# A two-layer transformer kernel: the second attention's out-projection, the last norm and the expert routing are laid into the attention, and the dispatch scatters wait after every eighth

## The chip, the cores and the metric

The kernel is one program on one core of a Trainium2 chip. Its engines are TensorE (PE, with its weight loads as PEld), VectorE (DVE), ScalarE (ACT), GpSimd (POOL) and SyncE (SP), which here issues most DMAs. The metric is the device time of one execution in microseconds (us), lower is better. The kernel before took 1064.49 us, the median of three runs (1061.39 to 1065.01).

## The reference, cut to what matters

Input x has 16 sequences of 256 tokens, 128 features: 4096 tokens. Two layers; each is an attention-like part and an expert part, both behind a layer norm with a scale and a shift per sequence, and both added back through a gate per sequence.

```python
h = _layernorm(x) * (1 + ca) + sa
x = x + ga * _L1_attn_ref(h, ...)     # 16 heads of 8, causal, relative positions, out = ctx @ w_o.T
h = _layernorm(x) * (1 + cb) + sb
x = x + gb * _L1_ffn_ref(h, ...)
# _L1_ffn_ref
gates = softmax(relu(xf @ Wr1 + br1) @ Wr2 + br2);  tg, ti = top_k(gates, 2)
out = silu(xf @ Ws1 + bs1) @ Ws2 + bs2              # shared expert, hidden 512
for e in range(8):
    out += w_e[:, None] * (silu(xf @ We1[e] + be1[e]) @ We2[e] + be2[e])
```

The first layer (a scan and eight small experts) is not touched by the change.

## The kernel before, in words

The work is cut in eight *chunks* of 512 tokens, two sequences each; for the attention of layer 1 a chunk is called a *pair*. The order of each engine's instructions is written out by hand, and semaphores join the engines.

**Attention.** `pair(i, k)` on PE runs 24 score banks twice: a first round whose row maxima DVE takes (`maxima`, L1188), a second whose exponentials ACT takes (`exponentials`, L799). Between the banks of the first round PE weights the values of pair i-1 (`weighted_values`, `weighted_relative`), and in the second it computes the relative scores of pair i+1, which DVE turns into bias tables (`bias_out`, L1178 and L1180). SP moves maxima (`move_maxima`), stores the contexts to DRAM (`store_values`, `store_relative`; the sums of the exponentials are one of nine rows of a head) and loads the next pair.

**Out-projection.** After all pairs SP loads sums, contexts and relative contexts back into SBUF (L540 to L554). DVE takes the reciprocal of the sums, PE spreads it over the features with a selecting matmul (`selp`, L1659), GpSimd adds the two contexts (`join`, L666), DVE multiplies (L1232), PE projects (L1671), DVE gates (`gated`, L948), GpSimd adds to x (`residual`, L618), and DVE takes mean and variance of a token (`statistics`, L888 and L891).

**Last norm and routing.** `layer_norm(3, ...)`: one square root for all tokens (ACT), normalised chunks (DVE, L936), transposes (PE, L1400), scale and shift (ACT, L728); with it the router: hidden layer (PE, L1699), transposed rows back (PE, L1681), logits (PE, L1711). Per group of two chunks DVE picks the two experts (`choose(g)`, L1013 to L1259), PE sums ranks over tokens (`ranks(g)`, L1688 and L1689), and DVE makes row numbers (`destinations(g)`, L1265 to L1271).

**Dispatch.** For each group g and each of the two picks k GpSimd issues eight indirect DMAs (scatters, L689) that write rows of x to their experts' places in DRAM: 64 scatters of 128 rows.

**Shared expert** (PE L1731 up, L1742 down; ACT L844 the silu; DVE L1318, L956, L959), then **experts**: 39 tiles of 256 rows, loaded by SP (L570, L573) once all scatters have landed, the shared expert is done and the tile table is there; GpSimd scatters the results (L697). Then a last stage weights and adds the two results of a token and stores the output.

Of the kernel before, what the change touches and what calls it, by code (L numbers as in the profile page):

```python
# [18 lines left out]
U32 = mybir.dt.uint32  # L19
ALU = mybir.AluOpType  # L20
# [3 lines left out]
P = 128  # L24
# [3 lines left out]
CH = 512  # L28
# [12 lines left out]
RANK_AT = 2  # L41
# [33 lines left out]
def build(nc, A, out):  # L75
    ctx = ExitStack()
    with ctx:
# [94 lines left out]
        R = Region(moe_base)  # L172
        Wr1 = R.take(32)
        Wr2 = R.take(E)
        br1 = R.take(1)
        RT1 = R.take(2 * CH).rearrange("p (s n) -> p s n", s=2)
        rowid = R.take(2 * NT).rearrange("p (k t) -> p k t", k=2)
        steps = R.take(2 * 64).rearrange("p (k n) -> p k n", k=2)
        below = R.take(P)
        restart = R.take(GE)  # L180
        reach = R.take(E * KT).rearrange("p (e k) -> p e k", e=E)
        ME, IN, EX = [R.take(NE).rearrange("p (g e t) -> p g e t", g=GROUPS, e=E) for _ in range(3)]
        tot = R.take(GROUPS * E).rearrange("p (g e) -> p g e", g=GROUPS)
        cum = R.take((GROUPS + 1) * E).rearrange("p (g e) -> p g e", g=GROUPS + 1)
        tiles, upto, spare = [R.take(E) for _ in range(3)]
        cmp, cmpd = [R.take(64 * E) for _ in range(2)]
        dest = [R.take(NT).bitcast(U32) for _ in range(2)]
        texp, tbase = [R.take(NG) for _ in range(2)]
        texpu, tbaseu = [R.take(NG).bitcast(U32) for _ in range(2)]
        ROWS = [R.take(NT * RW).rearrange("p (t n) -> p t n", t=NT) for _ in range(2)]  # L190
        W1S = R.take(W1W)
        W1 = R.take(UT * W1W).rearrange("p (s n) -> p s n", s=UT)
        moe_units = R.at
        HM1 = R.take(2 * KB1 * CH).rearrange("p (s k n) -> p s k n", s=2, k=KB1)
        R = Region(moe_units)
        HMT = R.take(2 * KB1 * GT).rearrange("p (s k n) -> p s k n", s=2, k=KB1)
        XR = R.take(UT * 2 * RW).rearrange("p (s r n) -> p s r n", s=UT, r=2)
        rid = R.take(UT * 2).rearrange("p (s r) -> p s r", s=UT).bitcast(U32)
        XT = R.take(2 * GT).rearrange("p (s n) -> p s n", s=2)
        YS = R.take(UT * GT).rearrange("p (s r n) -> p s r n", s=UT, r=2)  # L200
        YG = [r.rearrange("p t n -> p (t n)")[:, 0:NT * D].rearrange("p (t n) -> p t n", t=NT) for r in ROWS]


# [17 lines left out]
        BH, BL = [[R.take(P // 2 * BQ, BF16).rearrange("p (m q) -> p m q", q=BQ) for _ in range(2)] for _ in range(2)]  # L221
        PT = R.take(HS * PX).rearrange("p (h q) -> p h q", h=HS)
# [20 lines left out]
        R = Region(0)  # L243
        C1 = R.take(TOK)
        R1 = R.take(TOK)
        R = Region(early)
        DN = R.take(CH)
        DR = R.take(CH)
        DN7, DR7 = R.take(CH), R.take(CH)
        CX = R.take(2 * CH).rearrange("p (s n) -> p s n", s=2)  # L250
        selp = R.take(NP * P).rearrange("p (c n) -> p c n", c=NP)
        woT1 = R.take(D)
# [7 lines left out]
        rD = scratch("context_rel", [P, TOK])  # L260
        xsD = scratch("dispatched_rows", [AREA + SPARE * GT, RW])
# [54 lines left out]
        s_din7 = sem("s_din7")  # L316
# [23 lines left out]
        s_cin = [sem(f"s_cin{k}") for k in range(3)]  # L340
# [35 lines left out]

        def rank_bank(g):
            return bank[2 if g < 2 else 7]
# [12 lines left out]
        def _(sp):  # L391
# [136 lines left out]
            load_pair(1, 1)  # L528
            move_maxima(0, 0, 0)
# [5 lines left out]
            sp.wait_ge(s_r2, 24 * NP)  # L535
            for s, k in ((s_cst[0], 16 * 8), (s_cst[1], 16 * 8), (s_rst, 16 * 32)):
                sp.wait_ge(s, k * (NP - 1))
            part = (NP - 1) * CH
            values = cD.rearrange("(h v) t -> h v t", v=VW)
            sp.dma_start(DN[0:H * (NP - 1), :], values[:, HD, 0:part].rearrange("h (c t) -> c h t", c=NP - 1)  # L540
                         ).then_inc(s_din, 16)
            sp.dma_start(selp[:, :, :], A["selp"]).then_inc(s_wo, 16)
            sp.dma_start(woT1[:, :], A["woT1"]).then_inc(s_wo, 16)
            for k, (lo, hi) in enumerate(((0, 2 * CH), (2 * CH, part))):
                sp.dma_start(C1[:, lo:hi], values[:, 0:HD, lo:hi]).then_inc(s_cin[k], 16)
                sp.dma_start(R1[:, lo:hi], rD[:, lo:hi]).then_inc(s_cin[k], 16)
            store_values(NP - 1)
            for k in range(2):
                sp.wait_ge(s_cst[k], 16 * 8 * NP)
# [55 lines left out]
        def _(pool):  # L605
# [53 lines left out]
            for i in range(NP):  # L659
                neighbours(i)  # L660
                pool.wait_ge(s_nb, 2 * i + 2)
# [1250 lines left out]
```

## Time and profile before

| | us |
|---|---|
| median of three runs | 1064.49 |
| profiled execution, its own time | 1063.62 |
| its span, first to last instruction | 1061.6 |
| first layer, and the second's projections | 0 to 392 |
| attention, eight pairs | 392 to 655.2 |
| contexts back, out-projection, statistics | 655.2 to 708 |
| norm, routing, shared expert (and scatters, 737.8 to 829.9) | 708 to 858.6 |
| 39 expert tiles | 858.6 to 1029.7 |
| weighting, output | 1029.7 to 1061.6 |

PE is busy for 82% of the span, DVE for 57%, ACT for 33%, GpSimd for 23%. An average over the span hides the stages: PE has almost no idle time in the attention and with the expert tiles, and a good deal between the two. Times of the rows below are counted from the span's start.

### The profile page before, as it was taken

The numbers are of one execution on the slowest core, as the hardware profiler recorded it, in microseconds if no ns is written. First come the engines' busy times: TensorE is split into PE (matmuls) and PEld (weight loads), VectorE is DVE, ScalarE is ACT, GpSimd is POOL, SyncE is SP. The second block draws the span as 40 slices with busy tenths as digits, with TensorE's granted clock in tenths as the row PEclk, the third lists the DMA queues.
The fourth block names the chain that finished last, engine by engine and source line by source line (L and its number), as shares of the span: only waits on it lengthen the run. The fifth ranks groups of instructions, "written<-read, shape, count | busy, mean of one in ns | idle before, by whom it ended". The sixth has DMA issues, their size and how long they took to land.

```text
span 1061.6 us, 22575 instructions
## 1 busy us (share of the span) xinstructions
PE 870.2 (82%) x8768; PEld 601.6 (57%) x8768; DVE 608.5 (57%) x1613; ACT 352.2 (33%) x672; POOL 249.1 (23%) x251
## 2 busy tenths in 40 slices
PE   4875598999959699999999999855558879999960
PEld 3665265666635455665666565533336568888850
DVE  8781767666777887767776771474323222222217
ACT  1422021222241214553455345124121334344323
POOL 1030000000345400000000000521756204454443
PEclk9985699999979759999999996968578889999995
DMA  7993000000025712312231213610111036777747
GB/s 220 345 319 105 0 8 8 8 15 7 0 112 157 210 53 54 69 29 67 63 69 27 68 25 70 153 47 8 53 40 43 18 110 195 206 220 218 215 122 210
DMA packets 110363, 105.34 MB, mean 99 GB/s; under 512 B 47476, under 2 KB 100661, under 8 KB 109333
## 3 DMA queue, kind: packets, MB, share of 16 engines
q1 hardware_dynamic: 105733, 94.79, 32.2%
q0 software_dynamic: 4544, 9.35, 2.5%
q8 instruction: 60, 0.98, 0.4%
q14 instruction: 26, 0.21, 0.1%
HBM read 79.39 MB, written 44.51 MB: 117 GB/s over the span
## 4 chain that ended last, share of the span: by engine, by line
PE 60%; DVE 17%; issue 6%; DMA 6%; SPq 4%; ACT 3%; POOL 2%; another core or an unknown queue 1%; DVEq 0%; POOLq 0%
PE bank L1760 7%; PE bank L1770 6%; PE bank L1609 5%; PE bank L1447 5%; PE bank L1458 4%; PE bank L1459 4%; PE bank L1551 4%; PE bank L1503 4%; DVE sb_arena L1188 4%; PE bank L1742 3%; PE bank L1731 3%; PE bank L1529 3%; PE bank L1534 2%; DMA sb_arena<-in_iota 2%; SPq L470 1%
## 5 line engine op out<-in xcount | busy, mean ns | idle before, releaser
L1188 DVE TRANSPOSE_TENSOR_REDUCE sb_arena<-bank 128x16 f32<-128x512 f32 x192 | 120.4, 686 | 22.9 <-PE bank L1551 21.5
L799 ACT ACTIVATE sb_arena<-bank 128x512 f32<-128x512 f32 x192 | 99.1, 603 | 48.3 <-PE bank L1551 48.3
L697 POOL DMA_INDIRECT expert_results<-sb_arena x78 | 74.6, 957 | 125.1 <-DVE sb_arena L1340 109.6
L854 ACT ACTIVATE sb_arena<-bank,sb_arena 128x256 f32<-128x256 f32 x156 | 65.3, 472 | 102.4 <-PE bank L1760 101.7
L1447 PEld LDWEIGHTS bank<-sb_arena 128*128 128x128 f32 x512 | 67.3, 194 | 47.4 <-issue 25.4
L756 ACT ACTIVATE sb_arena<-bank 128x512 f32<-128x512 f32 x64 | 38.2, 597 | 151.2 <-PE bank L1459 151.2
L1760 PE MATMUL bank<-sb_arena 128*128 128x256 f32 x312 | 80.5, 402 | 6.7 <-DMA sb_arena<-in_w 2.7
L1447 PE MATMUL bank<-sb_arena 128*128 128x128 f32 x512 | 69.4, 279 | 16.1 <-DVE sb_arena L1099 16.1
L689 POOL DMA_INDIRECT dispatched_rows<-sb_arena x64 | 62.3, 973 | 62.6 <-DVE sb_arena L1271 44.0
L1770 PE MATMUL bank<-sb_arena 128*128 128x128 f32 x624 | 75.9, 274 | 0.0
L1081 DVE SCALAR_TENSOR_TENSOR sb_arena<-bank,sb_arena 128x128 f32<-128x128 f32 x256 | 71.7, 342 | 3.0 <-PE bank L1447 3.0
L1099 DVE TENSOR_TENSOR sb_arena<-sb_arena,bank 128x512 f32<-128x512 f32 x64 | 43.7, 685 | 51.4 <-ACT sb_arena L756 51.2
L1770 PEld LDWEIGHTS bank<-sb_arena 128*128 128x128 f32 x624 | 72.8, 191 | 0.1
L1609 PE MATMUL bank<-sb_arena 128*16 128x128 f32 x1024 | 68.0, 421 | 0.9 <-issue 0.9
L1760 PEld LDWEIGHTS bank<-sb_arena 128*128 128x128 f32 x312 | 58.1, 196 | 18.6 <-issue 9.1
L1458 PE MATMUL bank<-sb_arena 128*128 128x512 f32 x128 | 67.4, 609 | 0.0
L1503 PE MATMUL bank<-sb_arena 128*128 128x56 bf16 (+1 forms) x512 | 62.2, 281 | 5.5 <-DVE sb_arena L1168 3.2
L1459 PE MATMUL bank<-sb_arena 128*128 128x512 f32 x128 | 66.6, 602 | 0.0
L1178 DVE CAST sb_arena<-bank 128x512 bf16<-128x512 f32 x64 | 44.1, 689 | 38.5 <-PE bank L1503 38.5
L1551 PE MATMUL bank<-sb_arena,sb_identb 128*32 128x128 bf16 (+1 forms) x2304 | 64.9, 247 | 0.4 <-DVE sb_arena L1178 0.4
L1334 DVE CAST sb_arena<-sb_arena 128x2 uint32<-128x2 f32 x39 | 6.9, 178 | 98.6 <-DMA expert_results<-sb_arena 82.3
L652 POOL COPY sb_arena<-sb_arena 32x1024 f32<-32x1024 f32 x8 | 8.3, 1038 | 232.8 <-ACT sb_arena L799 232.8
(231 smaller groups left out, 1452.0 us busy)
## 6 DMA issues: line engine op xcount, KB each, us to landing
sb_arena<-in_w SPq DMA_DIRECT2D x39, 578.0 KB
dispatched_rows<-in_padding SPq DMA_DIRECT2D x8, 2064.0 KB, 34.9
sb_arena<-dispatched_rows SPq DMA_DIRECT2D x39, 129.0 KB
sb_GATE<-gates SPq DMA_DIRECT2D x2, 2048.0 KB, 7.1
sb_arena<-q_parts SPq DMA_DIRECT2D x8, 512.0 KB, 3.7
sb_arena<-k_parts SPq DMA_DIRECT2D x8, 512.0 KB, 5.1
context_rel<-sb_arena SPq DMA_DIRECT2D x256, 8.0 KB
sb_arena<-expert_results SPq DMA_DIRECT2D x16, 256.0 KB, 5.3
```

The source lines that it names most:

```text
L697: nc.gpsimd.indirect_dma_start(yD[:, :], bass.IndirectOffsetOnAxis(ap=rid[:, k, r:r + 1], axis=0), YS[:, k, r, :], None).then_inc(s_yo[k], 16)
L799: nc.scalar.activation(dst, src, ACT.Exp).then_inc(s_ex, 1)
L1081: ins = v.scalar_tensor_tensor(out=ACC[:, T, :], in0=src[:, t * D:(t + 1) * D], scalar=wstep[:, (j // NC) % 2, T:T + 1], in1=ACC[:, T, :], ...
L1188: v.tensor_reduce(dst.rearrange("p h b -> p (h b)"), bank[r % RING][:, :].rearrange("p (b c) -> p b c", c=32), AX, ALU.max, apply_transpos ...
L1447: ins = mm(bank[4 + j % 2][:, t * D:(t + 1) * D], HM0[:, j % 2, t * P:(t + 1) * P], W0[:, k, 2 * F0:3 * F0], start=True, stop=True)
L1458: mm(bank[j % 2][:, :], W0[:, k, 0:F0], chunk(hT, c), start=True, stop=True)
L1459: mm(bank[2 + j % 2][:, :], W0[:, k, F0:2 * F0], chunk(hT, c), start=True, stop=True).then_inc(s_up[0], 1)
L1503: ins = mm(out[:, :, :, x], GT4[:, first:first + 32, :].rearrange("p x a -> p (x a)"), queries[:, :, :, q], start=True, stop=True, skip_gr ...
L1551: ins = mm(dst[32 * b:32 * b + 32, :, 32 * b:32 * b + w], identb[:, 32 * a:32 * a + 32], src[:, :, :].rearrange("p (g b) q -> p g b q", g= ...
L1609: ins = mm(out[32 * j:32 * j + 2 * HD, :, x], relk[:, 32 * j + 8 * w + 2 * x:32 * j + 8 * w + 2 * x + 2, :], four, start=True, stop=True, ...
L1760: ins = mm(bank[2 * (k % 2) + b // 2][:, b % 2 * GT:(b % 2 + 1) * GT], W1[:, k, b * P:(b + 1) * P], XT[:, k % 2, :], start=True, stop=True ...
L1770: ins = mm(bank[6 + k % 2][:, r * D:(r + 1) * D], HMT[:, k % 2, b, r * P:(r + 1) * P], W1[:, k, I1 + b * D:I1 + (b + 1) * D], start=(b == ...
```

## The change

Nothing of the computation is changed but where the reciprocals of the sums are taken and how they are spread. What moves:

1. **Out-projection inside the attention.** `context_in(j)` on SP, right behind the stores of pair j, loads that pair's sums (as 128 x 64), its contexts and relative contexts, writes the reciprocals to DRAM and reads them back spread over the features, so the selecting matmul is gone. `context(j)` on GpSimd adds and multiplies, `project(j)` on PE stands in the second round of pair j+2, `gate_out(j)`, `sums(j+1)` and `statistics1(j)` stand in DVE's stream of pair j+2, `residual1(j)` in GpSimd's. So chunks 0 to 5 are done when the last pair's scores are.
2. **Norm and routing of chunks 0 to 5 beside the weighting of the last pair**, then the shared expert of the first chunks before chunks 6 and 7 have been normalised. The order is written out call by call on PE, ACT and DVE. The scatters start after `destinations(0)`, as before, and run beside the shared expert.
3. **GpSimd waits** before each group of eight scatters until all scatters so far have landed.

```diff
+            def context_in(j):
+                for k in range(2):
+                    sp.wait_ge(s_cst[k], 16 * 8 * (j + 1))
+                at = j * CH
+                values = cD.rearrange("(h v) t -> h v t", v=VW)[:, :, at:at + CH]
+                wait(sp, s_dr, j)
+                sp.dma_start(DN[:, :], values[:, HD, :].rearrange("h (s q) -> h s q", s=8)).then_inc(s_din, 16)
+                store_relative(j)
+                sp.wait_ge(s_dr, j + 1)
+                sp.dma_start(sD[j].rearrange("h (s q) -> (h s) q", s=8), DR[:, :]).then_inc(s_dst, 16)
+                if j >= 2:
+                    sp.wait_ge(s_y, NC + j - 1)
+                sp.dma_start(C1[:, j % 2, :], values[:, 0:HD, :]).then_inc(s_cin, 16)
+                sp.wait_ge(s_rst, 16 * 32 * (j + 1))
+                wait(sp, s_cr, j)
+                sp.dma_start(R1[:, :], rD[:, at:at + CH]).then_inc(s_cin, 16)
+                sp.wait_ge(s_dst, 16 * (j + 1))
+                wait(sp, s_cx, j)
+                sp.dma_start(DB[:, :], sD[j].unsqueeze(1).to_broadcast([H, HD, CH])).then_inc(s_db, 16)
...
                 load_values(i)
-                store_relative(i - 1)
+                context_in(i - 1)
...
             store_values(NP - 1)
...
+            context_in(NP - 1)
+            sp.wait_ge(s_rl, 4 * NP)
+            sp.wait_ge(s_nb, 2 * NP)
             sp.dma_start(W1S[:, :], A["w1s"]).then_inc(s_sw, 16)
...
             for i in range(NP):
+                if i >= 2:
+                    context(i - 2)
+                    residual1(i - 2)
                 neighbours(i)
...
                 for k in range(2):
+                    if g or k:
+                        pool.wait_ge(s_disp, 16 * GN * (2 * g + k))
                     pool.wait_ge(s_dest, 2 * g + k + 1)
                     for t in range(g * GN, (g + 1) * GN):
                         nc.gpsimd.indirect_dma_start(
...
                 if not last:
-                    bias_out(i + 1, 1 - k, range(1, BG))
+                    bias_out(i + 1, 1 - k, range(1, 4))
+                if i >= 2:
+                    gate_out(i - 2)
+                if not last:
+                    bias_out(i + 1, 1 - k, range(4, 6))
+                if i >= 1:
+                    sums(i - 1)
+                if not last:
+                    bias_out(i + 1, 1 - k, range(6, BG))
+                if i >= 2:
+                    statistics1(i - 2)
...
+            for c in range(5):
+                normalise1(c)
+            gate_out(6)
+            choose(0)
+            statistics1(6)
+            normalise1(5)
+            destinations(0)
+            choose(1)
+            sums(7)
+            last_context(7)
             destinations(1)
-            for g in range(2, GROUPS):
-                choose(g)
-                destinations(g)
+            choose(2)
+            gate_out(7)
+            last_residual(7)
+            statistics1(7)
+            destinations(2)
...
+            choose(3)
+            shared_out(4)
+            destinations(3)
...
+                    if part == 1 and i >= 2:
+                        pe.wait_ge(s_nm, 2 * i + 2)
+                        project(i - 2)
```

On DVE at the end of a pair in the middle of the attention, before (names: L1178 and L1180 are the bias tables, L1188 the first maxima of the next pair):

```order
L1178 CAST sb_arena<-bank5 128x64x8 [waits s_gen]
L1180 TENSOR_TENSOR sb_arena<-bank5,sb_arena 128x64x8 [waits s_bh]
L1178 CAST sb_arena<-bank6 128x64x8 [waits s_gen]
L1180 TENSOR_TENSOR sb_arena<-bank6,sb_arena 128x64x8 [waits s_bh]
L1188 TENSOR_REDUCE sb_arena<-bank0 128x16 [waits s_r1]
```

and now (L1261 and L1263 are the bias tables, L1312 the sums' reciprocal, L964 and L967 the statistics, L1271 the maxima):

```order
L1312 RECIPROCAL sb_arena<-sb_arena 128x64 [waits s_dst,s_din]
L1261 CAST sb_arena<-bank5 128x64x8 [waits s_gen]
L1263 TENSOR_TENSOR sb_arena<-bank5,sb_arena 128x64x8 [waits s_bh]
L1261 CAST sb_arena<-bank6 128x64x8 [waits s_gen]
L1263 TENSOR_TENSOR sb_arena<-bank6,sb_arena 128x64x8 [waits s_bh]
L964 BN_STATS sb_ST<-sb_X 128x6 [waits s_yr]
L964 BN_STATS sb_ST<-sb_X 128x6 x3
L967 BN_AGGR sb_MV<-sb_ST 128x2 [waits s_dv]
L967 BN_AGGR sb_MV<-sb_ST 128x2 x3
L1271 TENSOR_REDUCE sb_arena<-bank0 128x16 [waits s_r1]
```

The statistics of pair i-2 stand between the last bias table and the next pair's first maxima, and wait for GpSimd's residual.

On PE after the last pair's scores, before (L1581 and L1585 weight the values, L1609 the relative part, L1659 and L1671 the out-projection, L1400 the norm's transposes):

```order
L1585 MATMUL bank<-sb_arena 9x128 x4
L1609 MATMUL bank<-sb_arena 16x128 x64
L1659 MATMUL bank<-sb_arena 128x512 x2
L1671 MATMUL bank<-sb_arena 128x128 x4
L1659 MATMUL bank<-sb_arena 128x512
```

and now (L1744 relative part, L1803 transposes of the norm, L1809 router's hidden layer, L1816 rows back, L1829 logits, L1840 ranks, L1858 and L1868 shared expert up and down, L1755 projection), from the end of the last pair's weighting on:

```order
L1744 MATMUL bank<-sb_arena 16x128 x16
L1803 MATMUL bank<-sb_ident,sb_arena 128x128 x4
L1809 MATMUL bank<-sb_arena 32x512
L1816 MATMUL bank<-sb_ident,sb_arena 128x128 x4
L1829 MATMUL bank<-sb_arena 128x8 x4
L1840 MATMUL bank<-sb_arena 128x8
...
L1858 MATMUL bank<-sb_arena 128x512 x8
L1755 MATMUL bank<-sb_arena 128x128 x4
L1868 MATMUL bank<-sb_arena 128x128 x16
```

The norm's transposes of chunk 5 now follow the last relative part, and the last projection stands behind the shared expert's first two chunks.

On GpSimd, a scatter group before, and now:

```order
L689 DMA dispatched_rows<-sb_arena 34560x129 [waits s_dest]
L689 DMA dispatched_rows<-sb_arena 34560x129 x7
L689 DMA dispatched_rows<-sb_arena 34560x129 [waits s_dest,s_rows]
L689 DMA dispatched_rows<-sb_arena 34560x129 x7
L689 DMA dispatched_rows<-sb_arena 34560x129 [waits s_dest]
```

```order
L725 DMA dispatched_rows<-sb_arena 34560x129 [waits s_dest,s_disp]
L725 DMA dispatched_rows<-sb_arena 34560x129 x7
L725 DMA dispatched_rows<-sb_arena 34560x129 [waits s_dest,s_disp,s_rows]
L725 DMA dispatched_rows<-sb_arena 34560x129 x7
L725 DMA dispatched_rows<-sb_arena 34560x129 [waits s_dest,s_disp]
```

Only the wait for `s_disp`, which counts landed scatters, is new.

## Rows read from the trace of the kernel before

**Rows 1.** Stages: length, busy us of PE, PEld, DVE, ACT, POOL, clock, DMA share, GB/s

```profile
392.00:655.20 263.20, 256.85 (x5407) 161.02 (x5399) 186.60 (x309) 134.74 (x247) 17.42 (x17) 0.97 0.24 50
655.20:708.00 52.80, 37.62 (x336) 23.15 (x336) 27.49 (x96) 7.64 (x12) 21.97 (x18) 0.76 0.52 124
708.00:858.60 150.60, 104.29 (x482) 69.31 (x482) 51.93 (x191) 48.88 (x81) 62.26 (x64) 0.77 0.09 29
858.60:1029.70 171.10, 156.79 (x1014) 140.37 (x1014) 40.22 (x124) 65.33 (x156) 74.64 (x78) 0.97 0.67 195
```

**Rows 2.** The chain that ended last, 655 to 860: start, us, what

```profile
667.86 12.82 DMA context<-sb_XN
...
769.35 13.61 another core or an unknown queue
```

**Rows 3.** Timeline of DVE: start, us, engine line op, idle before and releaser

```profile
585.54 7.72 DVE L1188 TRANSPOSE_TENSOR_REDUCE sb_arena<-bank 128x16 f32<-128x512 f32 x12
...
684.68 0.75 DVE L948 TENSOR_TENSOR sb_TMP<-bank,sb_GATE 128x256 f32<-128x256 f32 x2
...
687.81 0.87 DVE L888 BATCH_NORM_STATS2 sb_ST<-sb_X 128x6 f32<-128x128 f32 x4
688.72 0.38 DVE L891 BATCH_NORM_AGGREGATE sb_MV<-sb_ST 128x2 f32<-128x6 f32 x4
...
724.64 0.22 DVE L1017 TENSOR_REDUCE sb_arena<-sb_arena 128x8 f32<-128x64 f32 x1 [4.34 <-ACT sb_arena L827]
...
729.53 2.14 DVE L936 TENSOR_SCALAR sb_XN<-sb_X,sb_MV,sb_RSTD 128x128 f32<-128x128 f32 x8
...
783.06 0.22 DVE L1265 TENSOR_TENSOR sb_arena<-sb_arena,bank 128x64 f32<-128x64 f32 x1 [13.71 <-remote]
```

**Rows 4.** Timeline of PE

```profile
587.50 0.39 PE L1529 MATMUL bank<-sb_arena 32*128 32x256 bf16 x2 [0.21 <-DVE sb_arena L1188]
...
664.22 7.90 PE L1609 MATMUL bank<-sb_arena 128*16 128x128 f32 x125
...
687.44 1.05 PE L1671 MATMUL bank<-sb_arena 128*128 128x128 f32 x8
...
745.40 1.11 PE L1400 MATMUL bank<-sb_ident,sb_XN 128*128 128x128 f32 x4 [6.55 <-issue]
...
751.60 0.58 PE L1689 MATMUL bank<-sb_arena,sb_ones 128*128 128x8 f32 x2
...
770.72 0.58 PE L1689 MATMUL bank<-sb_arena,sb_ones 128*128 128x8 f32 x2
...
787.55 5.77 PE L1731 MATMUL bank<-sb_arena 128*128 128x512 f32 x8 [10.98 <-ACT sb_arena L844]
...
837.22 3.73 PE L1742 MATMUL bank<-sb_arena 128*128 128x128 f32 x32
840.79 3.60 PE L1731 MATMUL bank<-sb_arena 128*128 128x512 f32 x8
```

**Rows 5.** Timeline of ACT

```profile
705.47 1.28 ACT L723 ACT_TABLE_LOAD   x1 [31.14 <-DVE sb_MV L891]
```

**Rows 6.** The scatters as one group: busy us, mean ns of one, idle before

```profile
L689 POOL DMA_INDIRECT dispatched_rows<-sb_arena x64 | 62.3, 973 | 62.6 <-DVE sb_arena L1271 44.0 <-issue 18.6
```

**Rows 7.** Timeline of GpSimd

```profile
784.83 0.96 POOL L689 DMA_INDIRECT dispatched_rows<-sb_arena  x1 [6.62 <-DVE sb_arena L1271]
...
817.30 1.27 POOL L689 DMA_INDIRECT dispatched_rows<-sb_arena  x1 [0.30 <-issue]
...
1028.67 0.96 POOL L697 DMA_INDIRECT expert_results<-sb_arena  x1 [0.30 <-issue]
```

**Rows 8.** Timeline of SP's queue

```profile
859.61 0.40 SPq L570 DMA_DIRECT2D sb_arena<-dispatched_rows  x1
...
1031.04 9.54 SPq L595 DMA_DIRECT2D sb_arena<-expert_results  x12
```

**Rows 9.** DMA issues, 656 to 708: KB each, median us to landing

```profile
sb_arena<-in_w1s SPq DMA_DIRECT2D x1, 578.0 KB, 3.7
```

More of the change, by code:

```diff
@@ L171, in build @@
         moe0_end = R.at
[L172 to L201, printed above, removed]
         R = Region(dense_base)
@@ new lines, in build @@
+        EX = R.take(NE).rearrange("p (g e t) -> p g e t", g=GROUPS, e=E)
+        tot = R.take(GROUPS * E).rearrange("p (g e) -> p g e", g=GROUPS)
+        cum = R.take((GROUPS + 1) * E).rearrange("p (g e) -> p g e", g=GROUPS + 1)
+        tiles, upto, spare = [R.take(E) for _ in range(3)]
+        cmp, cmpd = [R.take(NG * E) for _ in range(2)]
+        dest = [R.take(NT).bitcast(U32) for _ in range(2)]
+        texp, tbase = [R.take(NG) for _ in range(2)]
+        texpu, tbaseu = [R.take(NG).bitcast(U32) for _ in range(2)]
@@ L339, in build @@
         s_rst = sem("s_rst")
-        s_cin = [sem(f"s_cin{k}") for k in range(3)]
+        s_cin = sem("s_cin")
+        s_dst = sem("s_dst")
         s_wo = sem("s_wo")
@@ L1281, in _ @@
+            dve.wait_ge(s_wm[1], 16 * 10)
+            inverse_deviations(3, 0, 6)
             for k in range(2):
@@ new lines, in shared_down @@
+            def shared_down(c):
+                pe.wait_ge(s_sact, (c + 1) * KB1)
+                if c == 0:
+                    pe.wait_ge(s_dest, 3)
+                wait(pe, s_sout, c - 1)
+                for t in range(TPC):
+                    for b in range(KB1):
+                        ins = mm(bank[4 + c % 2][:, t * D:(t + 1) * D], HM1[:, c % 2, b, t * P:(t + 1) * P],
+                                 W1S[:, I1 + b * D:I1 + (b + 1) * D], start=(b == 0), stop=(b == KB1 - 1))
+                ins.then_inc(s_sdn, 1)
@@ new lines, in _ @@
+            last = NP - 1
+            norm_transposes(0)
+            weighted_values(last, range(0, 4))
+            norm_transposes(1)
+            route_hidden(0)
+            back(0)
+            weighted_values(last, range(4, 8))
+            norm_transposes(2)
+            route_hidden(1)
+            back(1)
+            logits1(0)
+            weighted_relative(last, range(0, 2))
+            norm_transposes(3)
+            route_hidden(2)
+            back(2)
+            logits1(1)
+            project(last - 1)
@@ new lines, in _ @@
+            weighted_relative(last, range(2, 6))
+            norm_transposes(4)
+            route_hidden(3)
+            back(3)
+            logits1(2)
+            weighted_relative(last, range(6, 8))
+            norm_transposes(5)
+            route_hidden(4)
+            back(4)
+            logits1(3)
+            ranks(0)
+            route_hidden(5)
+            back(5)
+            logits1(4)
+            logits1(5)
+            ranks(1)
+            shared_up(0)
+            shared_up(1)
@@ new lines, in _ @@
+            pe.wait_ge(s_re, 4 * NP)
+            project(last)
+            shared_down(0)
+            ranks(2)
+            shared_up(2)
+            shared_down(1)
+            shared_up(3)
+            norm_transposes(6)
+            shared_down(2)
+            norm_transposes(7)
+            shared_up(4)
+            route_hidden(6)
+            back(6)
+            shared_down(3)
+            route_hidden(7)
+            back(7)
+            shared_up(5)
+            logits1(6)
+            logits1(7)
```

522 lines of the change are left out of this document (297 added, 225 removed).

## The prediction

> **What bounds the kernel now.** I read the stages first [rows 1]. In the attention PE is busy 256.85 of 263.20 us, so there every added PE microsecond counts. In the two stages behind it, PE works 37.6 of 52.8 us and 104.3 of 150.6 us: 61.5 us idle in 203.4, and at a clock of 0.76 and 0.77 besides. The expert tiles keep PE busy 156.8 of 171.1 us. The change leaves them and everything before 392 us alone.
>
> The chain that ended last shows why PE idles in between [rows 2]: a landing of the last pair's contexts (12.82 us), then the norm, routing and a piece of 13.61 us that nothing in the kernel explains. In that piece DVE waits for ranks. PE had them at 771.3 (L1689) [rows 4], and DVE goes on at 783.06 [rows 3]. GpSimd had just scattered without pause; its next scatter starts at 784.83 [rows 7]. Such late starts come only while scatters run. So the change attacks two things: a serial stage, and late starts during long runs of scatters.
>
> **Attention, what is added.** PE: `project` is 8 matmul records, 1.05 us at the high clock (L1671) [rows 4]; it is in six pairs (i = 2 to 7), and PE has no gap to hide it: 6.3 us. Its semaphores are early: the contexts of i-2 were asked for at the end of pair i-1.
>
> DVE: in pairs 2 to 7 gating costs 0.75 us and statistics 0.87 + 0.38, with the link 1.3 us [rows 3]. DVE works 187 of 263 us, but its place decides. Gating falls between bias tables, where DVE waits for PE anyway: nothing. The reciprocal of 64 columns is not in the trace; I take 0.4 us on the path, bounded below by nothing (hidden between tables) and above by the 0.75 of a gating instruction with 256 columns, its nearest row. The statistics stand ahead of the next pair's first maxima, and there DVE is the bound: it runs 12 maxima without a gap (7.72 us) and PE waits for the first of them at 587.50 [rows 3, 4]. Five such transitions (2|3 to 6|7): 5 × (1.3 + 0.35) = 8.3 us, and 0.3 for the reciprocal in pair 1. Sum 14.9 us; bounds 6.3 (DVE catches up) and 22 (gating exposed too, 6 × 0.75, and 2 to 3 us of waits). I keep 14.9.
>
> SP: five more transfers and their waits per pair stand ahead of the next pair's loads. By SP's order they end some 3 to 5 us into the next pair, and the maxima's move, which PE needs at its second round, is due some 20 us in: hidden. This cover is priced as a rival. GpSimd gets 3 elementwise instructions in a stage where it works 17 of 263 us: nothing.
>
> **Behind the attention.** Let t be the time after PE's last score; before, that was 655.2, and the first tile load was issued at 859.61 [rows 8], t = 204.4. Now, following the orders:
>
> - To t = 4: the last exponential, the square root's table (1.28 us [rows 5]), reciprocal, normalising; PE waits.
> - To t = 34: weighting values and relative part (5.2 + 7.9 [rows 4] + a slow start of 2.6), with five transposes, four hidden layers, four row transposes, three logits and a projection between them, each 0.6 to 1.05 us, 13.2 in sum.
> - Chunk 5 isn't normalised before `choose(0)` has run, since DVE's stream has it so: relative copy 0.7, table load 1.28, exponential 0.3 (t = 36.4); picking takes 4.9 us (L1017 to the next normalising, 724.64 to 729.53 [rows 3]), statistics 1.3, normalising 1.1: t = 43.7. PE waits 9.5 us.
> - Transposes to ranks(0): 745.40 to 752.2 before, 6.8 us, the same list [rows 4]: t = 50.5. From ranks to a scatter takes 2 us (783.06 to 784.83 [rows 3, 7]): first scatter t = 52.5.
> - DVE: destinations(0) 1.7, shift 0.5, exponential 0.5, picking 4.9, then `sums(7)`: t = 59. Only now can SP write the last reciprocals, read them back spread, and issue the shared expert's weights, which lie over the score tables: 3 us of landings, then 3.7 [rows 9]. PE starts the shared expert at t = 66.
> - PE from there to ranks(3): seven up (the first at low clock, 5.77, the others 3.44: 840.79 to the end of 3.60 with the overlap off), five down (3.57: 837.22 to 840.79) [rows 4] = 44.2, and 8.7 for chunks 6 and 7, ranks and projection: t = 119.
> - `shared_out(4)` stands ahead of `destinations(3)` on DVE: its index is there at t = 122.3, and the scatter begins at 123.
> - Does GpSimd come later? A scatter costs 0.973 + 0.305 = 1.28 us, mostly 1.26 [rows 6]. What a wait adds is read at the end of the experts: last scatter started 1028.67, SP let go at 1031.04 [rows 7, 8]: 2.37 us, 1.1 more than a scatter's step. Six groups of eight and six waits from t = 52.5: 60.7 + 6.6, t = 120. So ranks, not the waits, decide by 3 us; five of the seven waits are free.
> - Two groups with a wait: 123 + 10.1 + 1.1 + 8.9 + 2.4 = 145.5, and SP 1.1 later: t = 146.6. PE's own rest (three down, one up, 14.2) ends at t = 134.
>
> The price of a wait has bounds: none (it falls where GpSimd waits for rows anyway), and 2.4 us if the step isn't overlapped, 7 × 2.4 = 17 us in all, of which the 3 us of slack take off some.
>
> Gain behind the attention 204.4 − 146.6 = 57.8; less 14.9 is 42.9. From the profiled execution's own 1063.62 (span 1061.6; the median is 0.9 higher) that is 1020.7. I add 2 for waits between engines that a hand schedule misses: **1023**.
>
> **Do the late starts go?** In 42.6 us of scatters beside the shared expert (787.5 to 829.9, but for 4.6) PE's eight chunks took 71.0 us (787.55 to 858.6) instead of 8 × 7.0 + 2.3 = 58.4, 12.6 lost; with the 11.8 of ranks(2) that is 24 us over 69 of scattering, 0.35 per us. The late starts seen lie some ten or more microseconds into a run of scatters (769, ACT and PE at 797 to 807 after a start at 784.83), hardly in its first eight. Now no run is longer than eight, about 10 us, with 1.1 us between. I expect most of them gone.
>
> By the Trainium skill (Runtime: NRT & Kernel Launch, section on instruction fetch mechanics) each sequencer fetches its next instructions by DMA through its own queue. If that fetch starved behind the scatters' descriptors, a pause would let it through, which favours the forecast; no row here shows such a fetch in the 13.6 us piece.
>
> **Rivals.**
> - *Late starts stay* (pause too short): the path from t = 52 to 122 loses 0.35 × 69 = 24 us: **1045**. For it: between 777 and 784.8 GpSimd paused 6.6 us, and DVE went on only towards its end. Against: the onset.
> - *Scatters slow down beside DVE.* Most scatters take 0.96 us, the one at 817.30, beside shared output on DVE, 1.27 [rows 7]. Now most lie beside such work. If all 64 cost 0.31 more, 20 us, less 3 of slack: **1040**. The Trainium skill (SBUF — State Buffer, the doors table and its "DVE blocks DMA" trap) says that DVE's two-port modes keep GpSimd from writing descriptors. The mean of 0.973 speaks against it.
> - *DVE catches up in the attention and the clock holds behind it*: 8 us of statistics and 4 to 8 of slow stretches fall away: **1010**.
> - *SP becomes the attention's bound*, the slower end. Its waits for landings are in its own stream; a context landing took 12.82 us beside bulk loads [rows 2], against 3 assumed. Then SP comes 10 us later into the next pair, its eight stores follow, and the maxima arrive after PE's second round is due. From 7 us per pair over six pairs (42.9 / 6) the gain is gone; at 10 us, 60: **1081**. Against: the bulk loads there moved seven chunks, here one.
> - *The wait does nothing*: ranks are always later than landings. That is nearly the forecast, and its time.
>
> **How the numbers follow.** Forecast 0.50 (own range 1012 to 1034), late starts stay 0.22, slow scatters 0.06, faster still 0.12, SP bound 0.06, a mixture of the second and the last or something unseen 0.04. A measurement here tells about 0.5%, 5 us, from no change. Faster by more: 0.88; within: 0.05; slower by more: 0.07. The range of 8 in 10 takes in rivals one and two and stops short of the tails: 1007 to 1050.
>
> **What would show it.** Each step: attention pairs 35.5 us before and some 38.2 after; first scatter about 52 us after the last score; a gap of near 1.1 us between eights; the shared expert's chunks at 7 us in the trace while scatters run; the last group starting behind ranks(3), not behind a landing. It would be wrong if pairs take over 40 us, if PE waits for SP's move of maxima, or if waits for an unknown queue of more than 5 us remain on ACT or DVE beside scatters.

## The result, and the profile after

The changed kernel took 1021.72 us (median of four runs, 1020.04 to 1026.58), the kernel before 1064.62 in the same session: ratio 0.961, 95% interval 0.957 to 0.965. The profiled execution took 1020.04 us, its span is 1018.2. The forecast was 1023.

I count t from PE's last score again: 661.3 now, 655.2 before. First the stages (start and end, length, then each engine's busy time, PE's granted clock, DMA share, GB/s), as in [rows 1]:

```profile
392.00:661.30 269.30, 259.90 (x5414) 163.15 (x5406) 198.25 (x373) 132.76 (x244) 37.93 (x34) 0.99 0.29 68
661.30:726.30 65.00, 39.00 (x380) 23.08 (x380) 22.88 (x97) 24.92 (x45) 13.55 (x13) 0.76 0.22 53
726.30:819.10 92.80, 73.24 (x374) 49.61 (x374) 39.63 (x131) 36.60 (x53) 54.31 (x56) 0.89 0.13 41
819.10:990.00 170.90, 153.37 (x1014) 138.79 (x1014) 36.79 (x117) 65.20 (x156) 74.62 (x78) 0.96 0.67 197
```

The attention is 6.1 us longer than before. Between the last score and the first tile load, 157.8 us are left of 204.4. From the first tile load to the last scatter of results (985.47, before 1028.67 [rows 7]) it is 166.4 us against 169.1, and from there to the end 32.7 against 32.9.

One transition between pairs on DVE, then on PE, which answers to [rows 3] at 585.54 and [rows 4] at 587.50:

```profile
589.48 0.86 DVE L964 BATCH_NORM_STATS2 sb_ST<-sb_X 128x6 f32<-128x128 f32 x4
590.38 0.38 DVE L967 BATCH_NORM_AGGREGATE sb_MV<-sb_ST 128x2 f32<-128x6 f32 x4
590.67 7.70 DVE L1271 TRANSPOSE_TENSOR_REDUCE sb_arena<-bank 128x16 f32<-128x512 f32 x12
```

```profile
587.99 1.10 PE L1662 MATMUL bank<-sb_arena 32*128 32x256 bf16 x8
591.42 0.39 PE L1662 MATMUL bank<-sb_arena 32*128 32x256 bf16 x2 [0.37 <-DVE sb_arena L1271]
592.61 0.39 PE L1662 MATMUL bank<-sb_arena 32*128 32x256 bf16 x2 [0.21 <-DVE sb_arena L1271]
```

The first PE row marks the end of a pair. In five pairs in a row it comes every 37.4 us; before, every 35.5. From it to the last matmul that waits for DVE it is 7.2 us (to 595.19), before 6.0. The statistics (0.86 + 0.38 us) delay the maxima by 1.2 us.

Behind the attention, PE in order of time:

```profile
704.49 1.12 PE L1803 MATMUL bank<-sb_ident,sb_arena 128*128 128x128 f32 x4 [9.61 <-DVE sb_arena L1339]
709.42 0.37 PE L1841 MATMUL bank<-sb_arena,sb_ones 128*128 128x8 f32 x2
726.33 1.22 PE L1858 MATMUL bank<-sb_arena 128*128 128x512 f32 x1 [7.87 <-DMA sb_arena<-in_w1s]
791.02 0.39 PE L1840 MATMUL bank<-sb_arena 128*128 128x8 f32 x2 [0.80 <-DVE sb_arena L1360]
```

These are the wait of 9.6 us for chunk 5's normalising, ranks(0) at t = 48, the shared expert's start at 65, and ranks(3) at t = 130. On GpSimd, the first scatters of five of the eights (within an eight they start 1.26 us apart, a few up to 1.5; the mean of one is 973 ns, as in [rows 6]), and SP's first tile load, which was at 859.61 in [rows 8]:

```profile
711.77 1.17 POOL L725 DMA_INDIRECT dispatched_rows<-sb_arena  x1 [24.18 <-DVE sb_arena L1373]
726.76 0.95 POOL L725 DMA_INDIRECT dispatched_rows<-sb_arena  x1 [4.92 <-DMA dispatched_rows<-sb_arena]
750.28 0.96 POOL L725 DMA_INDIRECT dispatched_rows<-sb_arena  x1 [1.60 <-DMA dispatched_rows<-sb_arena]
795.05 0.96 POOL L725 DMA_INDIRECT dispatched_rows<-sb_arena  x1 [11.59 <-DVE sb_arena L1373]
806.71 0.95 POOL L725 DMA_INDIRECT dispatched_rows<-sb_arena  x1 [1.58 <-DMA dispatched_rows<-sb_arena]
```

```profile
819.08 0.41 SPq L600 DMA_DIRECT2D sb_arena<-dispatched_rows  x1
```

The seventh eight waits for DVE's row numbers, not for landings, as the forecast had it. But late starts (instructions that begin although what they wait for has long been there) are not gone. The list of waits (us in total, times, longest) between 700 and 820 has:

```profile
DVE sb_arena L1377 <- remote: 28.4, 5, 11.7
ACT L877 <- remote: 7.9, 1, 7.9
DVE sb_arena L1094 <- remote: 7.2, 1, 7.2
ACT sb_arena L859 <- remote: 6.6, 1, 6.6
```

"remote" means that the profile shows nothing that ended the wait; the forecast calls it an unknown queue. Waits of more than 5 us for one, on ACT and DVE beside scatters, are what the forecast named as a sign of being wrong.

### The profile page after: what moved, and what is told of

The parts are those of the page before. It is cut to its first block, busy times and chain, and to the rows that moved or that the text cites. A ratio compares the mean times of both kernels' runs of the same rounds, so it can differ in the third digit from the quotient of the medians.

```text
span 1018.2 us, 22627 instructions
## 1 busy us (share of the span) xinstructions
PE 844.6 (83%) x8752; PEld 585.7 (58%) x8752; DVE 601.7 (59%) x1615; ACT 357.2 (35%) x677; POOL 255.3 (25%) x256
## 4 chain that ended last, share of the span: by engine, by line
PE 55%; DVE 20%; issue 6%; DMA 5%; POOL 4%; ACT 3%; SPq 3%; another core or an unknown queue 3%; DVEq 0%; POOLq 0%; ACTq 0%
PE bank L1947 6%; PE bank L1744 6%; PE bank L1957 6%; PE bank L1580 5%; PE bank L1591 5%; PE bank L1592 5%; DVE sb_arena L1271 4%; PE bank L1684 4%; PE bank L1636 3%; PE bank L1662 3%; DVE sb_ST L964 2%; ACT sb_arena L835 2%; DVE sb_arena L1261 2%; DMA sb_arena<-in_iota 2%
## 5 line engine op out<-in xcount | busy, mean ns | idle before, releaser
L1271 DVE TRANSPOSE_TENSOR_REDUCE sb_arena<-bank 128x16 f32<-128x512 f32 x192 | 120.3, 686 | 23.0 <-PE bank L1684 21.6
L835 ACT ACTIVATE sb_arena<-bank 128x512 f32<-128x512 f32 x192 | 99.1, 603 | 50.4 <-PE bank L1684 50.4
L930 ACT ACTIVATE sb_arena<-bank,sb_arena 128x256 f32<-128x256 f32 x156 | 65.2, 470 | 111.8 <-PE bank L1947 111.0
L1947 PE MATMUL bank<-sb_arena 128*128 128x256 f32 x312 | 77.9, 393 | 7.3 <-DVE sb_arena L1469 2.8
L1580 PE MATMUL bank<-sb_arena 128*128 128x128 f32 x512 | 70.0, 281 | 14.9 <-DVE sb_arena L1182 14.9
L1591 PE MATMUL bank<-sb_arena 128*128 128x512 f32 x128 | 69.1, 623 | 0.0
L1744 PE MATMUL bank<-sb_arena 128*16 128x128 f32 x1024 | 68.1, 423 | 0.0
L1592 PE MATMUL bank<-sb_arena 128*128 128x512 f32 x128 | 67.4, 609 | 0.0
L1261 DVE CAST sb_arena<-bank 128x512 bf16<-128x512 f32 x64 | 43.7, 682 | 37.0 <-PE bank L1636 37.0
L660 POOL TENSOR_TENSOR sb_TMP<-sb_arena,sb_GATE 128x256 f32<-128x256 f32 x16 | 11.3, 725 | 212.2 <-DVE sb_arena L1164 212.1
```

Of the source, the lines that this page charges most:

```text
L835: nc.scalar.activation(dst, src, ACT.Exp).then_inc(s_ex, 1)
L1271: v.tensor_reduce(dst.rearrange("p h b -> p (h b)"), bank[r % RING][:, :].rearrange("p (b c) -> p b c", c=32), AX, ALU.max, apply_transpos ...
L1580: ins = mm(bank[4 + j % 2][:, t * D:(t + 1) * D], HM0[:, j % 2, t * P:(t + 1) * P], W0[:, k, 2 * F0:3 * F0], start=True, stop=True)
L1591: mm(bank[j % 2][:, :], W0[:, k, 0:F0], chunk(hT, c), start=True, stop=True)
L1592: mm(bank[2 + j % 2][:, :], W0[:, k, F0:2 * F0], chunk(hT, c), start=True, stop=True).then_inc(s_up[0], 1)
L1744: ins = mm(out[32 * j:32 * j + 2 * HD, :, x], relk[:, 32 * j + 8 * w + 2 * x:32 * j + 8 * w + 2 * x + 2, :], four, start=True, stop=True, ...
```

## The experiments

All changes of time below are against the kernel before in the same session. In the next table, "PE stretch" is PE from its first matmul of the shared expert to the last of ranks(3), from each kernel's trace. In the rows from "ranks(3) early" on, up(6) of 3.4 us lies behind ranks(3) and no longer in the stretch, so that they compare with one another and not with those above.

| kernel | median us | ratio to before (95%) | PE stretch us |
|---|---|---|---|
| changed kernel | 1021.7 | 0.961 (0.957 to 0.965) | 65.2 |
| without the waits | 1040.5 | 0.981 (0.977 to 0.984) | 83.5 |
| before, with the waits | 1034.5 | 0.977 (0.973 to 0.980) | other order, see below |
| statistics in mid-pair | 1010.5 | 0.953 (0.949 to 0.956) | 58.8 |
| scatters held back | 1097.7 | one run | 52.5 |
| wait every four | 1029.0 | 0.966 (0.963 to 0.970) | 52.3 |
| chunk 5 first | 1015.3 | 0.952 (0.949 to 0.955) | 67.6 |
| ranks(3) early | 1023.5 | 0.960 (0.957 to 0.963) | 65.3 |
| the three edits | 1006.3 | 0.945 (0.942 to 0.947) | 58.4 |
| the same, wait every six | 1002.9 | 0.947 (0.943 to 0.951) | 52.1 |
| the same, short pause | 1016.1 | 0.959 (0.953 to 0.964) | 68.1 |
| the same, long pause | 1008.4; 1009.6 | 0.985 (0.982 to 0.988); 0.951 (0.945 to 0.957) | 49.8; 50.4 |

### The waits alone, and all but the waits

```diff
                 for k in range(2):
-                    if g or k:
-                        pool.wait_ge(s_disp, 16 * GN * (2 * g + k))
```

> The changed kernel without GpSimd's seven waits for landed scatters. Theory (the pauses keep the late starts short): scatters run 16 to 48 in a row, late starts between the shared expert's start and ranks(3) grow from about 11 us to the 24 us that before's rate gives, two waits' price of 1.6 us comes back: near 1032 us (1027 to 1040). Rival (the pauses do nothing; late starts are shorter only because less stands behind them): late starts stay near 11 us, the price of the last two waits goes: 1017 to 1021 us.

And the same two lines added to the kernel before:

> The kernel before with GpSimd's waits alone. In it the scatters end some 29 us ahead of the shared expert, so the waits' price (7 x 1.6 us) is hidden. Theory (the pauses keep late starts short): 24 us of late starts fall to some 10: near 1050 us (1045 to 1056). Rival (the pauses do nothing): 1062 to 1066 us, with waits of about 10 us for an unknown queue still on DVE or ACT.

Without them the time rises to 1040.5 us, just above the theory's range; alone, they take the kernel before from 1060.1 to 1034.5, below what either theory gave. The waits are worth 25.6 us there and 19 to 21 here (by the medians and by the ratios), the moved work without them 20 us. So about half of the gain comes from the seven waits. In the kernel before with waits the first tile load is at 831.22, 28.4 us earlier than in [rows 8]; 2.7 of these come from an attention that ended at 652.5 and not at 655.2. There PE runs the shared expert without any late start:

```profile
760.30:815.30 55.00, 55.00 (x299) 38.86 (x300) 24.03 (x75) 25.18 (x37) 37.21 (x39) 0.97 0.14 46
```

It ends at 818.69, in the kernel before at 858.54. That is 37 us less beyond the 2.7; then the scatters, whose last one starts at 827.83, set the end. So the late starts cost PE more in the kernel before than the 25.6 us that the waits gave back, and the price of the waits wasn't hidden, as the expectation had it.

What a late start looks like is plainest without the waits. PE, in the down projection of the shared expert, from a loop of 32 matmuls with no wait in it:

```profile
739.94 2.62 PE L1866 MATMUL bank<-sb_arena 128*128 128x128 f32 x22
...
747.81 0.37 PE L1866 MATMUL bank<-sb_arena 128*128 128x128 f32 x1 [2.43 <-issue]
750.62 0.37 PE L1866 MATMUL bank<-sb_arena 128*128 128x128 f32 x1 [2.43 <-issue]
753.41 0.37 PE L1866 MATMUL bank<-sb_arena 128*128 128x128 f32 x1 [2.42 <-issue]
756.22 0.37 PE L1866 MATMUL bank<-sb_arena 128*128 128x128 f32 x1 [2.44 <-issue]
...
759.71 0.81 PE L1866 MATMUL bank<-sb_arena 128*128 128x128 f32 x3 [1.03 <-issue]
```

and DVE in the same stretch:

```profile
735.92 0.28 DVE L1354 TENSOR_TENSOR sb_arena<-sb_arena 128x64 f32<-128x64 f32 x1 [0.55 <-DVE sb_arena L1086]
737.32 0.29 DVE L1355 TENSOR_TENSOR_SCAN sb_arena<-sb_arena 128x64 f32<-128x64 f32 x1 [1.12 <-DVE sb_arena L1354]
738.72 0.17 DVE L1357 TENSOR_TENSOR sb_arena<-sb_arena 128x8 f32<-128x8 f32 x1 [1.10 <-issue]
...
759.91 0.76 DVE L1321 TENSOR_TENSOR sb_arena<-bank,sb_GATE 128x256 f32<-128x256 f32 x2 [20.81 <-remote]
```

PE does one weight load and one matmul per 2.80 us, DVE one instruction per 1.40 us, then waits 20.8. PE's projection, which DVE waits for, had ended at 740.1. Both go on at 760, 5 us after the start of the last scatter of this run (754.26). PE's loop has no wait, and what DVE waits for was there: the engines look short of instructions, not of data. In the changed kernel PE shows the same 1.41 us grid (754.70, 756.11, 757.57, 758.98, 760.40), mostly two or three matmuls to a step. The two kernels have the same program on PE, and in both the third down projection slows from its 21st to 24th matmul on, at 754 in one and at 777 in the other: this speaks for the place in the program having a part in it, and not only the time since a run of scatters began.

### No scatters beside the shared expert

```diff
             pool.wait_ge(s_ids, 1)
+            pool.wait_ge(s_sdn, NC)
```

> The changed kernel, but GpSimd begins to scatter only when the shared expert is done on PE. The time is longer by the 64 scatters laid behind it (about 1080 to 1095 us) and tells nothing; what is read is PE from its first matmul of the shared expert to ranks(3), 64.7 us in the changed kernel. Theory (late starts come from scatters that run beside): 53 to 56 us, and no wait for an unknown queue above 1 us on ACT or DVE in this stretch. Rival (they come from code loading or the queues' own order, scatters or not): 62 to 66 us.

The theory holds: PE is busy throughout.

```profile
731.11:783.70 52.59, 52.59 (x269) 35.11 (x270) 27.15 (x96) 29.86 (x45) 0.00 (x0) 0.95 0.00 1
```

Nothing waits for an unknown queue from 700 to 820. So 52.5 us is the clean length of this stretch. The changed kernel loses 12.7 to late starts, the kernel without waits 31. In the changed kernel PE is idle for 7.2 of these 12.7 us; the rest are slower matmuls, at a granted clock of 0.91 in the stretch against 0.95 here. Without waits it is 22 idle and 9 slower, at 0.79.

### How often to wait

```diff
-                    if g or k:
-                        pool.wait_ge(s_disp, 16 * GN * (2 * g + k))
...
+                        if t % 4 == 0 and (g or k or t):
+                            pool.wait_ge(s_disp, 16 * (GN * (2 * g + k) + t % GN))
```

> The changed kernel with GpSimd waiting for all landings at every fourth scatter in place of every eighth. Without waits PE takes 83.1 us from the shared expert's start to ranks(3), with a wait every eight 64.7, with no scatters beside 52.1. Theory (what counts is how long scatters run without a pause): 53 to 59 us. GpSimd then pays 16 waits of 1.6 us and comes out of its sixth group at about t = 130, behind ranks(3), so scatters set the end: last one at t = 155, total 1018 to 1026 us. Rival (the number of scatters beside the shared expert counts, not the length of a run): 62 to 67 us and a total of 1023 to 1032 us.

```profile
730.15:782.60 52.45, 52.45 (x270) 35.03 (x270) 26.77 (x94) 29.96 (x45) 30.64 (x32) 0.95 0.12 39
```

The same 52.45 us as with no scatters, now with 32 of them beside it. The total of 1029.0 lies above the 1018 to 1026 expected: 15 waits (the edit leaves out the first scatter) make the 64 scatters last 107.3 us, the last one starts at t = 157.7, and they alone set the end.

### The statistics' place

```diff
                 row_maxima(i, 0)
+                if i >= 3:
+                    statistics1(i - 3)
                 maxima(i, range(16, 24))
...
-                if i >= 2:
-                    statistics1(i - 2)
```

> The changed kernel with the second norm's statistics of chunk i-3 in DVE's wait of 1.7 us ahead of the last eight maxima of a pair, in place of chunk i-2's at the end of the pair. Theory (at the pair's end they delay the first maxima, 1.2 us a pair in five pairs): pairs fall from 37.4 to near 36.2 us and the time by 5 to 6 us: near 1016 us. Rival (the pair is longer by the projection and its matmuls alone, and what the statistics delay is caught up): no change, 1020 to 1023 us. A third outcome: the wait of 1.7 us is itself on PE's path, the statistics delay the last maxima and so the exponentials: 1022 to 1026 us.

It took 1010.5 us, lower than any theory. Three of five pairs take 36.2 to 36.4 us against 37.4, as expected; the two others took 37.1 and 37.5, and the last score comes at 658.1. Five other profiles with the statistics at the pair's end have it at 664.4 to 667.4, and only the changed kernel's own at 661.3. The rest came behind the attention: its PE stretch is 58.8 us, not 65.2. How the runs of scatters meet the other engines' streams was not under my control, and I can't say how much of these 6 us belongs to the edit.

### Chunk 5 first, ranks(3) early, all three

```diff
             gate_out(6)
+            normalise1(5)
             choose(0)
             statistics1(6)
-            normalise1(5)
```

> The changed kernel with chunk 5's normalising on DVE ahead of choose(0) and the statistics of chunk 6. Theory (PE's 9.6 us wait ahead of ranks(0) is this place in DVE's stream): the wait falls to 1 to 3 us, ranks(0) and the first scatter come 5 to 6 us earlier, sums(7) and the shared expert's start some 4 us earlier; total 1015 to 1019 us. Rival (late starts, which depend on how the runs of scatters meet PE's and DVE's streams, shift and eat it): first scatter 5 us earlier, but PE from the shared expert's start to ranks(3) over 68 us and a total of 1020 to 1026 us.

The first scatter comes at t = 44.3 (50.5), the shared expert starts at 60.5 (65.1). 1015.3 us, as the theory had it, though the profiled run (span 1020.9, the slowest of the four) lost 2.4 us more to late starts.

```diff
             back(7)
-            shared_up(5)
             logits1(6)
             logits1(7)
+            shared_up(5)
             shared_down(4)
-            shared_up(6)
             ranks(3)
+            shared_up(6)
```

> The changed kernel with the logits of chunks 6 and 7 ahead of the shared expert's up(5), ranks(3) ahead of up(6), and on ACT and DVE the same turn (shares(3) ahead of hidden(5), destinations(3) ahead of shared_out(4)). Theory (the last scatters wait for ranks(3), and PE has slack behind it): ranks(3) some 7 us earlier, the seventh group starts when GpSimd is free (t near 124), last scatter near t = 146 against 154.5: total 1012 to 1016 us. Rival (late starts grow by as much, since more scatters fall beside the chain): 1018 to 1024 us.

The rival holds: ranks(3) at t = 129.6 against 129.8, although up(6), 3.4 us, no longer stands ahead of it. 1023.5 us, no gain.

> The three edits together: statistics in DVE's mid-pair wait (9 us in its own run), chunk 5 normalised first, ranks(3) ahead of up(6). Theory (each takes its own place on the path): near 1000 us, 996 to 1005. Rival (behind the attention they share one bound, GpSimd's 64 scatters with seven waits, 89 to 92 us from the first to the last): the first scatter at t near 46 puts the last at t near 137 and the tile loads at t near 140, which with pairs of 36.3 us gives 1000 us as a floor; if late starts take their share, 1004 to 1010 us.

1006.3 us, in the rival's range with late starts: ranks(3) at t = 117.9, last scatter 140.8, where 137 was the floor. PE's stretch is 8 us above the 50.4 of the long pause below, where no late start is left.

> The three edits together, with GpSimd's wait at every sixth scatter up to the 48th and one at the 56th (nine waits) in place of every eighth. A wait every four left no late start (52.3 us from the shared expert to ranks(3), as with no scatters beside), every eight left 12.6 us. Theory (the length of a run decides, with a threshold between four and eight, some 5 and 10 us): at six most late starts are gone, ranks(3) comes at t near 108, the scatters themselves set the end: from t = 43.4, 63 x 1.26 + 9 x 1.55 us, last one near t = 137 (140.8 with a wait every eight): total 1000 to 1004 us. Rival (only a pause within 5 us helps): ranks(3) at t = 115 or later and 1004 to 1010 us.

Late starts are mostly gone (52.1 us; two of 7.0 and 6.6 us on DVE are left, with slack behind them), and the scatters set the end: first at t = 43.5, last at 138.3. 1002.9 us is inside the theory's range. By the ratios this version and the one before it can't be told apart (0.947 and 0.945). Both beat the changed kernel by 1.5 to 1.8%.

### What the pause has to do

```diff
-                    if g or k:
-                        pool.wait_ge(s_disp, 16 * GN * (2 * g + k))
...
+                        if t % 4 == 0:
+                            n = (GN * (2 * g + k) + t % GN) // 4
+                            wait(pool, s_idle, n)
+                            nc.gpsimd.memset(idle[:, :], 0.0).then_inc(s_idle, 1)
```

> The three edits together without any wait for landings; ahead of every fourth scatter GpSimd instead clears 448 unused columns (some 0.4 us by the rows of its other clears: 4096 columns took 3.5 us). It is a pause shorter than the 1.6 us that a landing takes, so the queue of scatters doesn't run empty. Theory A (any break in the stream of descriptors lets the other engines' instructions through): as short as with the waits, ranks(3) at t = 105 to 112, last scatter near t = 131, total 995 to 1000 us. Theory B (the queue has to run empty): late starts as without waits, PE steps of 1.40 or 2.80 us, ranks(3) later than t = 125, total 1010 to 1025 us.

Theory B. GpSimd with the short pause, then PE, ranks(2):

```profile
704.56 0.96 POOL L729 DMA_INDIRECT dispatched_rows<-sb_arena  x1 [0.30 <-issue]
705.51 0.49 POOL L728 MEMSET sb_arena<- 128x448 f32 x1
706.17 0.96 POOL L729 DMA_INDIRECT dispatched_rows<-sb_arena  x1 [0.16 <-issue]
```

```profile
733.43 0.17 PE L1846 MATMUL bank<-sb_arena 128*128 128x8 f32 x1 [0.23 <-issue]
734.85 0.26 PE L1846 MATMUL bank<-sb_arena 128*128 128x8 f32 x1 [1.25 <-issue]
736.26 0.17 PE L1847 MATMUL bank<-sb_arena,sb_ones 128*128 128x8 f32 x1 [1.15 <-issue]
```

Then three clears in place of one (GpSimd's rows of the second run, and PE's stretch in it):

> As the one with the short pause, but three clears of 448 columns ahead of every fourth scatter (0.48 us each and 0.17 between: the next scatter begins some 2.1 us behind the last one's end, where a landing is complete 0.9 us behind it). No wait for landings. Theory (what helps is that the queue runs empty, not the wait): PE from the shared expert's start to ranks(3) falls from the 68.1 us of the short pause to 50 to 54, no late start above 3 us; 16 x 2.1 us of pauses make the scatters last 63 x 1.26 + 15 x 2.0 = 109 us, last one near t = 153: total 1014 to 1019 us, as the short pause for another reason. Rival (the wait itself, or its semaphore, is what helps): over 62 us, late starts of 8 us and more on DVE, total 1025 us or more.

> The kernel with the long pause once more, since on the chip of its first run the kernel before took 1024.6 us in place of 1059 to 1066, so that late starts may have been rare there whatever the pause. Where before takes some 1060 us again: theory (the queue running empty is what helps) 50 to 54 us from the shared expert's start to ranks(3), no late start above 3 us, 1005 to 1012 us; rival (the wait itself helps) over 62 us and 1018 us or more. Where before takes some 1025 us: the same 1006 to 1011 us, and the question stays open.

```profile
713.05 0.95 POOL L730 DMA_INDIRECT dispatched_rows<-sb_arena  x1 [0.30 <-issue]
713.99 1.55 POOL L729 MEMSET sb_arena<- 128x448 f32 x3
715.71 1.06 POOL L730 DMA_INDIRECT dispatched_rows<-sb_arena  x1 [0.16 <-issue]
```

```profile
717.50:767.90 50.40, 50.21 (x261) 33.97 (x261) 24.68 (x88) 28.01 (x42) 41.33 (x55) 0.92 0.13 42
```

PE's stretch falls from 68.1 to 50.4 us with no wait for a landing at all: the wait isn't needed, a pause does it. With 0.65 us at every fourth scatter, late starts take 17.7 us, with 1.7 us none. (The three edits without any pause were not run, so what 0.65 us alone gives is not known. The first long-pause session decides nothing here, since the kernel before took only 1024.6 us in it; the second does.) The last packet of a scatter ends 0.9 us behind the scatter's end (1.88 us from its start), so the two pauses lie on either side of the last packet: by the theory, it has to be through.

Another rival fits as well and no run here tells it from the theory: the mean step from scatter to scatter within a run. At 1.26 us (no waits) 31 us are lost, at 1.35 to 1.43 (short pause) 18, at 1.42 to 1.54 (every eight) 6 to 15 in five kernels, at 1.48 to 1.57 (every six) 2, at 1.6 and more (every four, long pause) none. A short pause at every scatter, with the same mean step as the long one, would decide it. Nor is the dose all: in the kernel before, a wait every eight left PE no late start.

## Why the prediction was right, point by point

**The total** was right by errors that offset each other, and in that by luck. The forecast had the first tile load at 655.2 + 14.9 + 146.6 = 816.7; it came at 819.08, with 8.8 us too much in the attention and 11.2 too little behind it. From there to the end it took 2.9 us less than before, where the forecast had no change but 2 us more for missed waits, so that 1023 ends up 1.3 above the median. What the forecast called a sign of being wrong, waits of over 5 us for an unknown queue on ACT or DVE beside scatters, is in the trace (11.7, 7.9, 7.2, 6.6): the time was right, the step on late starts was not.

**Attention, 14.9 us.** Too much: 6.1 in this profile. The pairs began 2.3 us early (the projections' first eight matmuls, at 317, took 3.67 us and not 5.37, at a granted clock of 1.00 and not 0.67; what stands there is the same in both kernels), and their own length grew by 8.4. A pair grew by 1.84 us, not 2.7: the statistics and the reciprocal cost 1.2 us and not 1.65, just what the statistics themselves take, so the 0.35 for the reciprocal was not on the path; the rest, projection and all, was 0.6 and not 1.05, and what takes up that difference is open. Over six profiles the attention's end is 6 to 12 us later than in the profile of before. The kernel before with waits, whose attention is the same as before's, ends it at 652.5, so the term lies between 6 and 15 us and 14.9 is at its upper end.

**To the first scatter.** t = 50.5, predicted 52.5; PE's wait for chunk 5 was 9.6 us, predicted 9.5; shared expert 65, predicted 66.

**Shared expert to ranks(3).** Predicted 53 us, and 52.5 is what it takes with no scatter beside it. Measured 65: the step that failed is that most late starts would go at a wait every eight. 12.7 us stayed, of 31. The reason given, that late starts begin ten microseconds into a run, does not hold: in the changed kernel PE's first slow step is at 754.70, 4.4 us into the eight that began at 750.28. At every four none is left, at every six nearly none.

**What the waits give.** The forecast put 24 us of late starts on the kernel before. The waits alone gave 25.6 there, and the agreement is luck. The 12.6 us of the shared expert count eight up projections behind 787.55, but the first ran at 771.14, so with the forecast's own lengths it is 16; and PE's 10.8 us ahead of ranks(2) at 770.26, 2.6 in the kernel with waits, are not counted. That makes 36 with the 11.8 of ranks(2), near the 37 by which PE's end moved, and the scatters with their waits took some 12 of it back.

**The price of a wait**, 1.1 us: 1.3 by the rows (idle 1.60 against 0.30), up to 1.9, and 4.6 for the first, which met the shared expert's weights. As predicted, ranks decide and not the waits, for the seventh eight (11.59 us for DVE).

**Rivals.** Late starts stay: two fifths of them did. Slow scatters: no, a scatter's mean is 973 ns before and after. SP as the bound: PE waited for no DMA between 392 and 661. The wait does nothing: refuted by 19 and 25.6 us.

**Instruction fetch.** The forecast named it without a row. The DMA queues of the kernel without waits between 714.7 and 759 (packets, MB, share of the 16 engines), with scatters running:

```profile
q0 software_dynamic: 1024, 2.12, 14.2%
q1 hardware_dynamic: 720, 1.41, 11.0%
```

and the same piece of the program with scatters held back (715.6 to 760):

```profile
q1 hardware_dynamic: 720, 1.41, 10.9%
q8 instruction: 1, 0.02, 0.1%
q14 instruction: 1, 0.01, 0.1%
```

That looks like a fetch kept out by scatters. Two things speak against it. In the first trace the two packets come at 760.86 and 761.12, when PE (759.71) and DVE (759.91) were already going again. And in the kernel before both kinds pass in the middle of an unbroken run of 32 scatters (738 to 778):

```profile
q0 software_dynamic: 992, 2.05, 15.7%
q8 instruction: 1, 0.02, 0.1%
q14 instruction: 1, 0.01, 0.1%
```

So the packets may be missing because the engines stand still, and not the other way round. By the Trainium skill (Runtime: NRT & Kernel Launch, section on instruction fetch mechanics) each sequencer streams its code in blocks through a DMA queue of its own, at a mostly hidden cost; no run here shows what that costs. The Trainium skill (DMA: Bandwidth & Descriptors, section on queues, rings and completion order) has each DMA engine take turns between the queues with work, a packet at a time; by that a fetch would pass between two scatters, and the rows of the kernel before agree. What holds the engines up while scatters run stays open: that it is the supply of instructions is argued from the even steps in a loop without waits, and no run here changed the code's size or place to test it.

## What to carry to other kernels

Where an engine's instructions start late beside a stream of GpSimd scatters, put a pause of some 1.7 us behind every four to six scatters, by a wait for their landings or by other work of that length. It costs only where the scatters themselves set the end. Count late starts before moving work: ranks(3) early was to free 7 us and lost them all to late starts.

## What was not expected of the hardware

- Engines that start late beside scatters run on a grid of 1.40 us: without waits, one instruction on DVE, a weight load and a matmul per 2.80 us on PE.
- The kernel before took 1054 to 1067 us in five sessions and 1021.8 to 1026.9 us (seven runs) in one. The some 36 us between are about the 37 that PE lost to late starts in the kernel before; no trace shows that kernel at the lower time, so whether late starts are missing there stays open. In that one session the long pause gained 1.5% over before, elsewhere 4.9%.
- PE's clock dips within the attention: two pairs of the kernel without waits took 37.9 and 38.3 us at a granted clock of 0.95 and 0.96, their neighbours 37.4 at 1.00. The other four profiles whose last score comes at 664.9 to 667.4 have such pairs too (37.7 to 38.6 us), not all of them at a lower clock.
